# A post-norm decoder layer on one core: the hand-written call order of all five engines drawn up anew

## The reference, cut to what matters

```python
x = _layernorm(x + _L0_attn_ref(x, ...))            # Mamba-2 block: in projection, conv over 4 taps,
                                                     # silu, decay matrix per head, masked product, out projection
x = _layernorm(x + _L0_xattn_ref(ctx_1024, x, ...))  # attention: latents x, keys and values from
                                                     # context (120 rows) and x (256 rows), 8 heads of 64
x = _layernorm(x + _L0_ffn_ref(x, ...))              # 3 cycles: out = out + coupling(out) * twist(out)
```

## Time and profile before

| what | value |
|---|---|
| runs | 3862.89, 3863.9, 3865.1 us (median 3863.9) |
| profiled execution, its span | 3861.4 us |
| PE busy | 3783.3 us, 98% of the span |
| DVE, ACT, POOL busy | 3286.2, 3237.9, 1748.5 us |
| granted clock of PE | full in all but the first and the last slice of the span |
| table loads on ACT | 445, seven in a round |

### The profile page before, as it was taken

The page is one execution under the profiler, slowest core; times in us unless marked ns, Lnnn a source line. Parts: engine busy times, 40 slices in busy tenths (PEclk is TensorE's granted clock), DMA queues, the critical chain, the costliest instruction groups (busy, mean ns, idle before and its releaser), DMA issues.

```text
span 3861.4 us, 77375 instructions
## 1 busy us (share of the span) xinstructions
PE 3783.3 (98%) x25728; PEld 3000.9 (78%) x25728; DVE 3286.2 (85%) x8098; ACT 3237.9 (84%) x7812; POOL 1748.5 (45%) x3084
## 2 busy tenths in 40 slices
PE   6999999999999999999999999999999999999997
PEld 5777877877877878778778778777787787787775
DVE  7888888888888888888888888888888888888874
ACT  5788888888888888888888888888888888888885
POOL 3444445354454444453544544534535445445442
PEclk8999999999999999999999999999999999999998
DMA  3111112111211111121111111111211211111110
GB/s 97 54 47 59 55 45 61 54 42 58 58 45 55 48 59 54 45 61 53 43 57 59 45 55 50 56 55 45 61 55 42 61 55 45 55 54 53 55 38 17
DMA packets 312350, 203.14 MB, mean 53 GB/s; under 512 B 55056, under 2 KB 310928, under 8 KB 311952
## 3 DMA queue, kind: packets, MB, share of 16 engines
q1 hardware_dynamic: 311952, 198.20, 17.5%
HBM read 180.17 MB, written 17.96 MB: 51 GB/s over the span
## 4 chain that ended last, share of the span: by engine, by line
PE 59%; ACT 16%; DVE 15%; issue 4%; POOL 4%; DMA 1%; SPq 0%; DVEq 0%; POOLq 0%
PE psum L253 20%; PE psum L428 8%; PE psum L338 6%; PE psum L463 5%; PE psum L438 5%; PE psum L452 4%; PE psum L325 4%; ACT prob L979 3%; ACT h L1021 2%; ACT L979 2%; ACT L1021 2%; PE psum L497 2%; ACT xc L891 2%; POOL rs_mix L2175 2%; DVE nmax L1638 1%
## 5 line engine op out<-in xcount | busy, mean ns | idle before, releaser
L979 ACT ACTIVATE prob<-psum,nmax 128x376 f32<-128x376 f32 x1024 | 585.2, 575 | 49.5 <-DVE nmax L1638 46.2
L1638 DVE TENSOR_REDUCE nmax<-psum 128x1 f32<-128x376 f32 x1024 | 541.5, 540 | 14.4 <-PE psum L428 11.0
L2139 POOL TENSOR_TENSOR Lm<-Lm,G 128x384 f32<-128x384 f32 x512 | 506.1, 1012 | 92.8 <-DVE out_sb L1741 68.4
L438 PE MATMUL psum<-ident,prob 128*128 128x128 f32 (+1 forms) x3072 | 480.5, 276 | 2.1 <-ACT probT L989 1.1
L1442 DVE SCALAR_TENSOR_TENSOR u<-psum,par,u 128x253 f32<-128x253 f32 (+5 forms) x960 | 449.1, 479 | 28.1 <-ACT u L882 1.7
L428 PE MATMUL psum<-kT,q_sb 64*128 64x376 f32 x2048 | 467.7, 528 | 0.2 <-ACT prob L979 0.2
L438 PEld LDWEIGHTS psum<-ident,prob 128*128 128x128 f32 (+1 forms) x3072 | 363.0, 141 | 73.9 <-issue 45.0
L989 ACT ACTIVATE probT<-psum 128x384 f32<-128x384 f32 x512 | 252.7, 494 | 182.7 <-PE psum L438 182.5
L2126 POOL TENSOR_SCALAR_AFFINE_SELECT Lm<-Lm 128x256 f32<-128x256 f32 x512 | 205.7, 435 | 411.6 <-DMA Lm<-cum_row 411.6
L253 PE MATMUL psum<-x_hi,w_in_hi 128*128 128x256 f32 (+1 forms) x1152 | 360.9, 313 | 22.5 <-DVE w_in_lo L1764 9.3
L452 PE MATMUL psum<-probT,V 128*64 128x256 f32 (+1 forms) x3072 | 375.0, 385 | 0.3 <-ACT probT L989 0.3
(11 more groups left out here) (222 smaller groups left out, 11157.9 us busy)
## 6 DMA issues: line engine op xcount, KB each, us to landing
Lm<-cum_row SPq DMA_DIRECT2D x64, 1024.0 KB, 5.2
Lm<-cum_row SPq DMA_DIRECT2D x64, 512.0 KB, 6.5
invT<-inv_row SPq DMA_DIRECT2D x256, 128.0 KB, 3.0
xT_sb<-in_xT SPq DMA_DIRECT2D x64, 256.0 KB, 3.1
x_sb<-in_x SPq DMA_DIRECT2D x64, 256.0 KB, 3.3
result<-out_sb SPq DMA_DIRECT2D x64, 256.0 KB, 2.2
inv_row<-inv_t SPq DMA_DIRECT2D x512, 1.0 KB
ctx_sb<-in_ctx SPq DMA_DIRECT2D x64, 120.0 KB, 2.7
```

Of the source, the lines that this page charges most:

```text
L438: t = tr(banks[b][0:m, j * P:(j + 1) * P], prob[:, r, j0:j0 + m], ident[:, :])
L979: act(prob[:, r, :], b[:, 0:NK], ACT.Exp, bias=nmax[:, n:n + 1], accum_out=psum_row[:, n:n + 1]).then_inc(a_exp, 1)
L1638: e.tensor_reduce(nmax[:, n:n + 1], banks[bank_of["sc", s, n]][:, 0:NK], AX.X, ALU.max, negate=True).then_inc(d_max, 1)
L2139: t = tt(Lm[:, h, :], Lm[:, h, :], G[:, :], ALU.mult)
```

## The change

No helper is changed; no instruction is added or removed; the wait conditions and the buffers are the same. All five lists of calls are written in another order, prologue, round and epilogue. The change is described as keeping operations of DVE and POOL that share something apart, and chains of operations whole. The body of the loop is also cut at another point of the period: on PE a round now begins at `turn(f, 14)`, on DVE at `bcdt(m)`, so that the letters f, a, m on DVE, POOL and SP now stand for a sequence one earlier than they did at the same moment. Line numbers of ACT and of what follows grow by two and more.

PE's round, cut to the three places that the text below speaks of (first half, the feed-forward chain, the end):

```diff
             for p in range(2, NSEQ - 1):
                 f, a, m = p - 2, p - 1, p
-                xcT(m, 1)
+                turn(f, 14)
+                in_z(m, 1)
+                turn(f, 15)
+                layer(f - 1, 2, 2)
+                values(f, 2)
+                values(f, 3)
                 scores(a, 0, 1)
+                layer(f - 1, 2, 3)
                 q_pair(a, 1)
+                w_o(f, 0)
                 cb(m)
+                ctxT(m)
                 scores(a, 1, 0)
-                w_o(f, 0)
-                in_z(m, 1)
-                scores(a, 1, 1)
                 v_tile(a, 0)
                 w_o(f, 1)
+                k_tile(a, 3)
                 turn(a, 0)
...
                 layer(f, 1, 1)
+                turn(a, 10)
                 k_tile(m, 0)
                 layer(f, 1, 2)
-                turn(a, 10)
+                turn(a, 11)
+                xcT(m + 1, 0)
+                xcT(m + 1, 1)
+                layer(f, 1, 3)
                 k_tile(m, 1)
-                layer(f, 1, 3)
-                turn(a, 11)
                 in_z(m + 1, 0)
+                scores(m, 0, 0)
                 turn(a, 12)
                 k_tile(m, 2)
-                scores(m, 0, 0)
-                xcT(m + 1, 0)
                 turn(a, 13)
                 layer(f, 2, 1)
```

More of the change, by code:

```diff
@@ L597, in _ @@
[L597 to L605, removed]
             y_pair(1, 2)
             y_pair(1, 3)
+            scores(0, 2, 1)
+            bcdt(2)
+            turn(0, 2)
+            in_x(2, 0)
+            turn(0, 3)
+            v_tile(0, 1)
+            v_tile(0, 2)
+            mean_square(1)
+            turn(0, 4)
@@ L608, in _ @@
+            scores(0, 3, 0)
+            out_proj(1)
+            turn(0, 5)
+            in_x(2, 1)
+            scores(0, 3, 1)
+            turn(0, 6)
+            values(0, 0)
+            turn(0, 7)
+            x1T(1)
+            values(0, 1)
+            turn(0, 8)
+            q_pair(1, 0)
             turn(0, 9)
-            bcdt(2)
             turn(0, 10)
-            scores(0, 3, 1)
-            out_proj(1)
-            mean_square(1)
+            k_tile(1, 0)
             turn(0, 11)
-            values(0, 1)
+            k_tile(1, 1)
@@ L616, in _ @@
+            xcT(2, 0)
+            xcT(2, 1)
+            k_tile(1, 2)
             turn(0, 12)
+            in_z(2, 0)
+            scores(1, 0, 0)
             turn(0, 13)
[L618 to L629, removed]
             for p in range(2, NSEQ - 1):
@@ L646, in _ @@
                 turn(a, 1)
-                ctxT(m)
-                k_tile(a, 3)
                 turn(a, 2)
+                scores(a, 2, 0)
                 y_pair(m, 2)
@@ L699, in _ @@
-                values(a, 2)
-                values(a, 3)
-                layer(f, 2, 3)
-            last = NSEQ - 1
-            scores(last - 1, 0, 1)
-            xcT(last, 1)
-            k_tile(last - 1, 3)
[L706 to L713, removed]
+            last = NSEQ - 1
+            turn(last - 2, 14)
@@ new lines, in _ @@
+            turn(last - 2, 15)
+            in_z(last, 1)
+            layer(last - 3, 2, 2)
+            values(last - 2, 2)
+            values(last - 2, 3)
+            scores(last - 1, 0, 1)
+            cb(last)
+            layer(last - 3, 2, 3)
+            q_pair(last - 1, 1)
+            w_o(last - 2, 0)
+            scores(last - 1, 1, 0)
+            v_tile(last - 1, 0)
+            w_o(last - 2, 1)
+            scores(last - 1, 1, 1)
+            turn(last - 1, 0)
+            ctxT(last)
@@ L725, in _ @@
[L725 to L728, removed]
+            y_pair(last, 3)
+            v_tile(last - 1, 1)
+            x2_turn(last - 2)
+            scores(last - 1, 3, 0)
+            v_tile(last - 1, 2)
+            turn(last - 1, 4)
+            layer(last - 2, 0, 0)
             turn(last - 1, 5)
-            glob(last - 2, 0)
-            layer(last - 2, 0, 0)
-            turn(last - 1, 6)
             mean_square(last)
@@ L734, in _ @@
             out_proj(last)
-            v_tile(last - 1, 2)
+            layer(last - 2, 0, 1)
+            glob(last - 2, 0)
+            scores(last - 1, 3, 1)
+            values(last - 1, 0)
+            glob(last - 2, 1)
+            turn(last - 1, 6)
+            layer(last - 2, 0, 2)
+            x1T(last)
             turn(last - 1, 7)
-            glob(last - 2, 1)
-            layer(last - 2, 0, 1)
             turn(last - 1, 8)
-            turn(last - 1, 9)
+            layer(last - 2, 0, 3)
@@ new lines, in _ @@
+            cum(last)
+            mean_square(last - 1)
+            turn_out(last - 2, 4)
+            kv_split(last - 1, 0)
+            top(last - 2, 13)
+            out_norm(last - 4, 0)
+            x1_raw(last - 1)
+            turn_out(last - 2, 6)
+            x1_norm(last - 1)
+            by_token(last)
+            kv_split(last - 1, 1)
+            base(last - 3)
+            out_norm(last - 4, 1)
+            turn_out(last - 2, 8)
+            cycle(last - 3, 0)
+            conv(last, 2)
@@ L2101, in _ @@
             out_norm(last, 1)
-            out_norm(last, 0)
         @block.gpsimd
```

1150 lines of the change are left out of this document (576 added, 574 removed).

## The result

The changed kernel takes 3928.5 us (median of 4 runs, 3927.5 to 3930.4) against 3863.8 for the kernel before: a ratio of 1.0167, 95% interval 1.0153 to 1.0182. It is slower by 65 us, where 3819 was forecast. The span of its profiled execution is 3926.7 us.

A forecast was written before the change was run, and what follows sets the result against it. PE, busy 98% of the span, was taken as the bound. Terms of -0.66 us a round times 61 gave -40 us, the ends -5: 3816.4 us of span, plus 2.5 for the median, 3819 us; range 3787 to 3868.

The forecast's parts named there:

- what DVE and POOL share: DVE's `out_norm`, stretched while POOL works: 0.7 us a round of DVE time saved at most, nothing on the path.
- the wait ahead of `layer(f, 2, 1)`: PE's wait for ACT's gelu, 0.35 us, falls to 0.2: -0.15 us a round, bounds -0.35 and 0.
- Neighbours: PE calls take different times by what stands beside them; seven places change: -0.2 us a round, bounds -0.4 and +0.1.
- `k_tile(m, 1)`: PE's wait for the bank that ACT's `k_out(m, 0)` drains goes wholly: -0.20 us a round.
- `x_low`: PE's `bcdt(m + 1)` no longer late behind DVE's `x_low(m + 1)`, so longer rounds go: -0.11 us a round, bounds -0.11 and 0.
- The ends: Prologue -5 us, bounds -10 and +4; epilogue 0, bounds -4 and +5.
- C: Rival: `divide(a, 1)` on DVE comes too late for PE's `w_o(f, 0)`; slower, 3876 us; chance 0.14.
- B: Rival: ACT's `conv_th(m + 1, 1)` ahead of `layer(f, 1, 1)` delays PE's `layer(f, 1, 2)`, 0.6 us a round; about 3860 us; chance 0.10.

The follow-up runs named there:

- guard_both: The changed kernel with one wait more on POOL: `times_g(m, 0)` also waits for the last operation of `out_sum(f - 1, 0)`; 3911.8 us, ratio 1.0123.
- sums_only: Changed kernel, both `out_sum` a round later ahead of `turn_out(f, 14)`, `x2_raw`, `x2_stats` ahead of `top(a, 3)`, `x_low` behind `gate_silu(m, 1)`, `conv_th` unmoved; 3854.6 us.
- the best kernel: Changed kernel, `out_sum` pair a round later, `x2_raw`, `x2_stats` ahead of `top(a, 3)`, `x_low` behind `gate_silu(m, 1)`, `conv_th(m + 1, 0)` behind `exp(a, 12)`; 3828.0 us.

## Why the prediction was wrong

**What failed.** The step "what DVE and POOL share", which put the whole of it at nothing on the path; it cost 0.9 us a round ahead of `w_o(f, 1)`. It named the condition ("it costs only if the cover goes, that is, if DVE becomes late at one of the places below") and did not look whether the new order meets it. I read `out_norm`, the operation whose stretching the change removes (403/406/411 ns in the changed kernel), and not `out_sum`, the one it brings into the open. The row was in the trace of the kernel before:

```profile
L1741 DVE SCALAR_TENSOR_TENSOR out_sb<-x,of_minus,out_sb x102: 343/416/488, 542.4 to 3492.8; 128x128 f32<-128x128 f32 x102
```

up to 488 ns where the plain one takes 343. With it the new order could be read: `out_sum(f - 1, 0)` now directly behind `out_sum(f - 1, 1)`, POOL's wait on the latter alone, POOL free to start `times_g` in the middle, and `x2_raw(f, 0)`, which holds a bank of PE, two calls behind. Those long rows are not chance: all 51 are those of the `out_sum` that comes second, and they end 0.14 us behind a half of POOL's `masked` (DVE, then POOL):

```profile
1724.98 0.49 DVE L1741 SCALAR_TENSOR_TENSOR out_sb<-x,of_minus,out_sb 128x128 f32<-128x128 f32 x1
```

```profile
1724.45 0.87 POOL L2126 TENSOR_SCALAR_AFFINE_SELECT Lm<-Lm 128x256 f32<-128x256 f32 x2
```

Its price by runs: 0.9 us a round from the stretching ahead of `w_o(f, 1)` alone (guard_both), 74 us with its followers (the changed kernel, 3928.5, against sums_only, 3854.6). That second number is not of the collision alone: sums_only also frees POOL's chain, moves `x_low`, and sets `x2_raw` ahead of `top(a, 3)`.

The Trainium skill (SBUF — State Buffer, Who interferes with whom) says that a DVE operation with two inputs in SBUF contends with a GpSimd one that reads SBUF, and that the later one is blocked for the whole of the other. L1746 has two such inputs and agrees: 0.34 us alone, 1.11 when begun 0.16 us behind a half of `times_g` that takes 1.12. Which of the two comes first can't be read from the rows to 0.02 us: L1746 is the blocked one in the 17 rounds too in which its row starts that little ahead. `x2_raw`, with one input in PSUM, takes 0.41 to 0.43 us in all 100 cases, 89 of them beside a `times_g`, and `top`, a reduction from PSUM, 0.51 to 0.55 everywhere. I had cited the page for the gain of `out_norm` only.

**The second miss** is in the part on the wait ahead of `layer(f, 2, 1)`: "`bcdt_th` and one `conv_th` left the stretch ahead of it". They did, and I counted the relief and not where `conv_th(m + 1, 0)` went: ahead of `exp(a, 12)`, which holds a score bank. 0.58 us a round, 22 to 27 us in the runs.

**The terms, one by one** (starts in the changed kernel's trace):
- Neighbours, forecast -0.2 a round. `in_z(m, 1)` takes 1.49 us (1.50 forecast), `w_o(f, 0)` 1746.88 - 1745.35 = 1.53 (1.54), `k_tile(a, 3)` pays the 0.10 foreseen; `cb` and `ctxT` take 1747.57 - 1746.88 = 0.69 together, 0.28 over what they took apart (0.35 was the worst price). `w_o(f, 1)` takes 1.64 right behind its wait, and 1.54 in the best kernel, where it has none. Right as a whole, but the prediction's bound for it is not what its terms give: without the price of `cb` and `ctxT` they add up to -0.49, not -0.4.
- `k_tile(m, 1)`, forecast -0.20: it starts 0.37 us behind `layer(f, 1, 3)`, which is that call's own time, and `turn(a, 10)` takes 0.24. Right.
- `layer(f, 2, 1)`, forecast -0.15: `turn(a, 13)` takes 0.71 us, of which 0.23 stands as idle, where 0.68 was the earlier trace rows and 0.53 was forecast. Wrong by 0.18. ACT's `k_out(m, 0)` did start earlier, 0.04 us behind the end of `k_tile(m, 0)` where it was 0.21, so in the new order ACT's run hangs on PE's own call and starts no sooner by what leaves the stretch ahead of it. The wait stayed all the same.
- `x_low`, forecast -0.11: it releases nobody on PE in the loop. Right as to its place. What I did not see is that it then meets `times_g` (761 ns in the median for 687, and `times_g` 1.45 us for 1.0).
- The ends, forecast -5: about +6. `x1T(2)` starts 0.3 us earlier than before, so the prologue gave nothing. From the start of the last `x1T` on, the changed kernel takes 3926.7 - 3813.3 = 113.4 us and the one before 3861.4 - 3755.8 = 105.6: it is the epilogue, put at 0 with +5 at most, that is longer by some 7.8, and it is as long in the best kernel. PE has these two waits there (releaser, us in total, times, longest), where the kernel before has no wait of `turn` for `turn_out` and 0.4 us at L475:

```profile
PE psum L438 <- ACT probT L991: 2.2, 1, 2.2
PE psum L475 <- DVE x L1435: 2.1, 2, 1.5
```

No run tests this, and why they arise stays open. The stated upper end of the range, 3868, had left that +5 out too.

Together: 59.93 us, less 1.10 at `v_tile`, 0.13 at `w_o(f, 1)` and 0.58 at `scores(a, 3, 1)`, leaves 58.1, where I forecast 58.3. The best kernel, with these waits taken away, has 58.16. So the sum of what the change does was right to 0.2 us, and two waits that it brings were not in it, nor the 0.13 at `y_pair(m, 3)`. That the sum is so near is partly luck: the -0.15 ahead of `layer(f, 2, 1)` did not come, and smaller savings of which no term spoke took its place (the 16 `turn` together take 0.40 us less, only 0.20 of it foreseen). `scores(a, 3, 1)` keeps 0.07 of its 0.58 in the best kernel.

**The rivals.** C had the sign and the neighbourhood (`w_o`, `cb`, POOL's chain), but the wrong link: `divide(f, 1)` was in time, `w_o(f, 0)` did not wait, `w_o(f, 1)` did. The queue it named, `times_g` up to `y_pair`, was indeed next, once the collision was mended. B had the right kind of fault in the wrong one of two `conv_th`: `layer(f, 1, 2)` takes 0.45 us, as before. The far side of C, which I cut from the range, is where the result lies.

## What to carry to other kernels

When an order is redrawn, follow each operation that holds a PSUM bank back through its queue to everything ahead of it, and ask of each of these how long it takes at its new place, beside what the neighbouring engine now runs. A wait that lets the other engine begin must be read again in the new order: here it named the first `out_sum` of the two in both orders, but before, four other calls of DVE stood between the two, and now none does. And a mend of a late operation is tested on what it pushes back: letting `x2_raw` go first cost 31 us, one wait more on the other engine gave 17, and moving the colliding work to where the other engine rests made 0.9% under the kernel before.

## What the runs showed of the hardware

A blocked DVE operation shows no idle time: it is a busy row of 1.1 us in place of 0.34 that ends 0.15 us behind the other engine's instruction, and the view of waits names only the next in the chain. Both sides pay: `x_low` took up to 1366 ns in the kernel with the guard (684 alone), and single `times_g` halves up to 1459 (1005). A matmul call right behind a wait of PE was itself slower here, `w_o(f, 1)` 1.64 against 1.54 us.
